# Three edits to a one-core layer kernel: per-tile score waits, expert groups in pairs on one ring of copy places, split products from chunk 6

## The chip, the cores and the metric

The kernel runs on one core of a Trainium2 chip. The core has five engines that run their own instruction queues in order: TensorE (PE), VectorE (DVE), ScalarE (ACT), GpSimd (POOL) and SyncE (SP), which here only issues transfers. The metric is the device time of one execution in microseconds (us).

## What is computed

A transformer layer for 4 batches of 128 tokens with 512 features: cross-attention to a context of 2048 rows of 384 features per batch, causal self-attention with 16 heads over low-rank projections, then a mixture of experts (4 shared blocks and 16 routed experts, 4 per token), each with a residual. Cut to what the change touches:

```python
query = einsum('bqi,ih->bqh', x, Wq) + bq
key   = einsum('bkt,th->bkh', ctx, Wk) + bk
value = einsum('bkt,th->bkh', ctx, Wv) + bv
weights = softmax(einsum('bqh,bkh->bqk', query, key) / sqrt(512))
x = x + einsum('bqk,bkh->bqh', weights, value)
# ... self-attention, then for each token its 4 experts e with weights c_e:
x = x + shared(x_norm) + sum(c_e * down_e(relu(up_e(x_norm)) ** 2))
```

The kernel folds Wk into the query and Wv behind the sum, so that scores are products with the context itself, and the second product is weights by context.

## The kernel before, in words

**Cross-attention.** The context comes in G = 16 chunks of 512 rows (4 per batch), each twice: transposed (`ring_T`, 4 places, three tiles t = 0, 1, 2 of 128 x 512) for the scores, and as it lies (`ring`, 3 places) for the product with the weights. One loop, written out alike on every engine, runs steps 1 to 20. In step s, chunk s is prepared, the scores of chunk s-1 are computed, and chunk s-5 (LAG = 5) goes through its second product. "Split" operands are a high part, rounded by a copy to the type float32r, and a low part, the rest; a split product is three matmuls (`split_mm`, L1580).

- ACT makes the high parts of a chunk (`chunk_hi`, L747) and DVE the low ones (`chunk_lo`, L1281); in steps 2 to 4 POOL makes the low part of tile 2 (L614). PE (`chunk_scores`, L1846) waits for all low parts of the chunk, then runs 9 matmuls. DVE moves the scores out (L1392), ACT takes the exponential (`chunk_weights`, L826).
- PE turns the weights (`chunk_T`, L1843) into bank B_W, ACT copies that to `wT` (L894, two places), and PE multiplies `wT` by `ring` in plain fp32 (L1898), four products per chunk.
- From step 8 on the same loop carries the work of finished batches: the normalised sums and their projection (`sums_hi`, `sums_lo`, `attended`), norms (`cross_added`, `normalise`, with a root on POOL, L598 and L620), `compress`, `keys_and_queries`, `values`. From step 13 (U_STEP) on it carries one self-attention unit per step: `pair_scores` (L1726, two units at a time), mask and maximum on DVE (`mask_and_max`, L1092 to L1100), `unit_exp` on ACT (L852), `unit_weights` on POOL (L627), `unit_T` on PE (L1748, into B_W too) and `unit_copy` on ACT (L841). In step 17, ACT and DVE also split the output weights W_O (L734, L1055).

The order of each engine's calls within a step is that of its loop: ACT at L880, DVE at L1352, PE at L1868, POOL at L642, the loads of SP at L507.

**Experts.** NG = 20 groups of 4 slots of 32 tokens. For each group PE turns the gathered tokens (`group_rows_T`, L2012), runs the up products (`group_up`, L2043), turns the hidden values (`group_hidden_T`, L2054) and runs the down products (`group_down`, L2075). Up and down products run as four column strips of 32, the transposes on the whole array. From group 4 (GS) on the experts are chosen at run time; the weights of slots 1 to 3 are first copied to fixed places, 4 for up and 4 for down (slots 1 and 2 by DVE, L1507 and L1514; slot 3 by ACT, L1016 and L1024). PE's loop (L2091) runs, per group, up(g), hidden_T(g-1), rows_T(g+2), down(g-2). At the end `last_shared` (L2086), 32 matmuls (L2113, L2114) and DVE's sums (L1559, L1563) close the output.

Of the kernel before, what the change touches and what calls it, by code (L numbers as in the profile page):

```python
# [36 lines left out]
def layer_program(nc, x, ctx_in, ctxT_in, wqT, wkT, wv, wd, wu, woT, experts, bq, bk, bv, gate, bias_e,  # L37
# [41 lines left out]
    with ExitStack() as es:  # L79
# [99 lines left out]
        ring_T = at("ring_T", [P, RING_T, TC, CHUNK], ring_at + RING * KT * TD * 4)  # L179
        sc = at("sc", [P, 2, NKEY], s_at)  # L180
# [69 lines left out]
        NC = 4  # L250
        up_copy = [at(f"up_copy{i}", [P, HALF], xT_at + i * HALF * 4) for i in range(NC)]
        down_copy = [at(f"down_copy{i}", [P, HALF], (ring_at, hw_at)[i // 2] + i % 2 * HALF * 4) for i in range(NC)]
# [106 lines left out]
        ulo_first, dlo_first = sem("ulo_first"), sem("dlo_first")  # L359
        u_lo_pool, d3_in = sem("u_lo_pool"), sem("d3_in")  # L360
# [51 lines left out]

        def pool_parts(g):
            return sum(q <= g for q in POOL_LO)
# [30 lines left out]
        def copy_no(g, q):  # L445

            return (NQ - 1) * (g - GS) + q - 1

        def place(g, q):
            return copy_no(g, q) % NC  # L450

        def last_user(g, q):

            n = copy_no(g, q) - NC
            return GS + n // (NQ - 1) if n >= 0 else None
# [5 lines left out]
        def _(sp):  # L461
# [19 lines left out]
            def load_chunk_T(g):  # L481
                if g >= RING_T:
                    sp.wait_ge(cTlo_ok, low_parts(g - RING_T))
                    if pool_parts(g - RING_T):
                        sp.wait_ge(cTlo_pool, pool_parts(g - RING_T))
                sp.dma_start(ring_T[:, g % RING_T], ctxT_in[g].rearrange("p (t n) -> p t n", t=TC)).then_inc(ctxT_at[g % RING_T], 16)
# [33 lines left out]
            load_expert(0)  # L520
            load_expert(1)
# [49 lines left out]
        def _(pool):  # L571
# [157 lines left out]
        def _(act_e):  # L729
# [17 lines left out]
            def chunk_hi(g, t):  # L747
                if t == 0:
                    act_e.wait_ge(ctxT_at[g % RING_T], 16 * (g // RING_T + 1))
                if g >= 2 and t == 0:  # L750
                    act_e.wait_ge(s_mm, g - 1)
                copy(cT[:, g % 2, 0, t, :], ring_T[:, g % RING_T, t, :]).then_inc(cThi_ok, 1)  # L752
# [75 lines left out]

            def attended_hi(b):
# [50 lines left out]
            for step in range(1, TAIL):  # L880
# [9 lines left out]
                if 0 <= g < G:  # L890
                    act_e.wait_ge(wT_mm, g + 1)
                    if g >= 2:
                        act_e.wait_ge(o_mm, g - 1)
                    copy(wT[:, g % 2, :], bank[B_W][:]).then_inc(wT_ok, 1)  # L894
# [113 lines left out]
            def copy_up(g, expert):  # L1008
                q = NQ - 1
                if g == GS:  # L1010
                    act_e.wait_ge(up_mm, IC * NSH)
                    for i in range(GS):
                        act_e.wait_ge(wx_in[i], 16 * NQ)
                if (v := last_user(g, q)) is not None:
                    act_e.wait_ge(hs_up, v + 1)
                copy(up_copy[place(g, q)][:], WX[:, bass.ds(expert * (2 * HALF), HALF)]).then_inc(up_third, 1)  # L1016

            def copy_down(g, expert):
                q = NQ - 1
                if g == GS:  # L1020
                    act_e.wait_ge(acc_mm, NSH - 1)
                if (v := last_user(g, q)) is not None:
                    act_e.wait_ge(ys_mm, v + 1)
# [1144 lines left out]
```

## Time and profile before

| | us |
|---|---|
| median of 3 runs (lowest, highest) | 355.23 (354.63, 355.56) |
| the profiled execution | 355.39 |
| its span, first to last instruction | 353.7 |
| PE busy in the span | 336.4 (95%) |
| DVE busy | 240.7 (68%) |
| ACT busy | 189.4 (54%) |
| POOL busy | 95.6 (27%) |

The mean granted TensorE clock is 0.99 of full speed. Busy PE time counts a matmul from its start to its modelled end, and ends overlap the next starts; what a matmul costs in a row of them is the distance between starts. The chunk loop's 20 steps lie between about 36 and 160 us, the groups of the experts between 248 and 340 us.

### The profile page before, as it was taken

Reading aid. Unit: us, or ns where it says so; the run is one execution under the profiler, and the core shown is the slowest. Engines: PE = TensorE matmul, PEld = TensorE weight load, DVE = VectorE, ACT = ScalarE, POOL = GpSimd, SP = SyncE. Lnnn points to the kernel's source line nnn. Section 1 sums busy time; section 2 is a strip of 40 time slices with the busy share of each in tenths; the row PEclk is TensorE's granted clock in tenths of the full one; section 3 lists DMA queues with packets and bytes.
Section 4 is the critical chain, followed back from the end, with each engine's and each line's share of the span. In section 5 each row is a group of like instructions: output and inputs, shape, how many; then the busy total and the mean of one; then the engine's idle time right before and its main releaser. Section 6 shows DMA issues by size and latency. Waiting matters only on the chain.

```text
span 353.7 us, 7041 instructions
## 1 busy us (share of the span) xinstructions
PE 336.4 (95%) x2554; PEld 235.2 (67%) x2554; DVE 240.7 (68%) x475; ACT 189.4 (54%) x428; POOL 95.6 (27%) x114
## 2 busy tenths in 40 slices
PE   6999889999999999999899899999999999999996
PEld 4998656677777766767789789787544444444344
DVE  2875869665489728748975469980547777778486
ACT  2356666533577476565777454402246777777520
POOL 3600310000001311226575140004457544432000
PEclk9899999999999999999899999999999999999999
DMA  6984398985333227118023470799835633321663
GB/s 232 400 336 165 139 396 356 418 290 216 120 126 111 92 90 259 69 39 348 0 89 124 149 267 16 294 380 391 341 110 184 196 120 120 121 92 61 238 268 119
DMA packets 17185, 69.70 MB, mean 197 GB/s; under 512 B 2816, under 2 KB 3328, under 8 KB 14592
## 3 DMA queue, kind: packets, MB, share of 16 engines
q1 hardware_dynamic: 12768, 56.93, 43.0%
q0 software_dynamic: 3520, 11.54, 9.4%
q10 hardware_dynamic: 864, 0.79, 0.7%
q8 instruction: 21, 0.34, 0.4%
q14 instruction: 12, 0.10, 0.1%
HBM read 61.91 MB, written 7.34 MB: 196 GB/s over the span
## 4 chain that ended last, share of the span: by engine, by line
PE 76%; DVE 12%; ACT 6%; issue 3%; DMA 2%; POOL 0%; ACTq 0%; DVEq 0%
PE bank L2075 10%; PE bank L2043 10%; PE bank L1582 8%; PE bank L1898 8%; PE bank L1584 8%; PE bank L1583 8%; PE bank L2012 3%; PE bank L1791 2%; PE bank L2054 2%; PE bank L2086 2%; DMA raw<-in_wkT 2%; DVE cT L1283 2%; PE bank L1748 2%; PE bank L1843 2%; PE bank L1589 1%
## 5 line engine op out<-in xcount | busy, mean ns | idle before, releaser
L1898 PE MATMUL bank<-ring,wT 128*128 128x384 f32 x128 | 44.0, 487 | 0.7 <-ACT wT L894 0.7
L2075 PE MATMUL bank<-WX,hsT 128*32 128x512 f32 (+1 forms) x128 | 38.2, 598 | 0.0
L2043 PE MATMUL bank<-WX,xsT 128*32 128x256 f32 (+1 forms) x256 | 37.9, 380 | 0.0
L1283 DVE TENSOR_TENSOR cT<-ring_T,cT 128x512 fp32r<-128x512 f32 x45 | 31.0, 732 | 6.7 <-ACT cT L752 6.7
L1898 PEld LDWEIGHTS bank<-ring,wT 128*128 128x128 f32 x128 | 23.6, 190 | 14.2 <-ACT wT L894 0.9
L2043 PEld LDWEIGHTS bank<-WX,xsT 128*32 128x32 f32 x256 | 17.9, 110 | 21.0 <-issue 10.7
L1514 DVE COPY down_copy<-WX 128x1024 f32 x32 | 21.0, 695 | 15.8 <-PE bank L2075 15.8
L2075 PE MATMUL bank<-down_copy,hsT 128*32 128x512 f32 x192 | 30.7, 598 | 0.0
L752 ACT CAST cT<-ring_T 128x512 fp32r<-128x512 f32 x48 | 27.0, 619 | 6.5 <-PE bank L1584 6.3
L2043 PE MATMUL bank<-up_copy,xsT 128*32 128x256 f32 x384 | 30.4, 379 | 0.0
L688 POOL DMA_INDIRECT xs<-x_rows,from_row x20 | 20.0, 1001 | 37.1 <-DVE to_row L1237 25.2
L598 POOL TENSOR_TENSOR rstd<-var,mhalf 128x1 f32<-128x1 f32 x12 | 7.5, 626 | 72.3 <-DVE var L1069 72.3
L695 POOL DMA_INDIRECT y_rows<-ys,to_row x16 | 17.1, 1068 | 33.7 <-ACT ys L1000 33.7
L1507 DVE COPY up_copy<-WX 128x1024 f32 x32 | 21.1, 696 | 7.4 <-PE bank L2043 3.5
L1024 ACT COPY down_copy<-WX 128x1024 f32 x16 | 16.8, 1049 | 17.1 <-PE bank L2075 17.1
L1492 DVE COPY xsT<-bank 128x512 f32<-128x512 f32 x20 | 13.7, 685 | 14.8 <-PE bank L2012 14.8
L1582 PE MATMUL bank<-cT,qk_h 128*128 128x512 f32 x48 | 20.2, 420 | 2.4 <-DVE cT L1283 1.7
L1016 ACT COPY up_copy<-WX 128x1024 f32 x16 | 16.8, 1048 | 4.7 <-PE bank L2043 3.4
L1584 PE MATMUL bank<-cT,qk_l 128*128 128x512 f32 x48 | 18.8, 392 | 0.0
L1583 PE MATMUL bank<-cT,qk_h 128*128 128x512 f32 x48 | 18.8, 392 | 0.0
L2075 PEld LDWEIGHTS bank<-WX,hsT 128*32 128x32 f32 x128 | 7.4, 109 | 16.5 <-issue 16.5
L1582 PE MATMUL bank<-xT_l,u_w 128*128 128x256 f32 (+2 forms) x56 | 17.9, 320 | 0.0
(296 smaller groups left out, 892.3 us busy)
## 6 DMA issues: line engine op xcount, KB each, us to landing
WX<-in_experts SPq DMA_DIRECT2D x16, 1024.0 KB, 7.0
ring_T<-in_ctxT SPq DMA_DIRECT2D x16, 768.0 KB, 6.8
ring<-in_ctx SPq DMA_DIRECT2D x16, 768.0 KB, 5.0
WX<-y_rows SPq DMA_DIRECT2D x4, 1024.0 KB, 9.4
raw<-in_experts SPq DMA_DIRECT2D x3, 1024.0 KB, 4.8
raw<-in_wqT SPq DMA_DIRECT2D x4, 256.0 KB, 5.6
res<-in_x SPq DMA_DIRECT2D x4, 256.0 KB, 7.8
raw<-in_woT SPq DMA_DIRECT2D x1, 1024.0 KB, 4.9
```

The costliest lines, as they stand in the source:

```text
L688: nc.gpsimd.indirect_dma_start(out=xs[:, s % NXS, :], out_offset=None, in_=x_rows, in_offset=bass.IndirectOffsetOnAxis(ap=from_row[:, s:s ...
L695: nc.gpsimd.indirect_dma_start(out=y_rows, out_offset=bass.IndirectOffsetOnAxis(ap=to_row[:, s:s + 1], axis=0), in_=ys[:, s % NYS, :], in_ ...
L752: copy(cT[:, g % 2, 0, t, :], ring_T[:, g % RING_T, t, :]).then_inc(cThi_ok, 1)
L1283: V_.tensor_tensor(cT[:, g % 2, 1, t, :], ring_T[:, g % RING_T, t, :], f32(cT[:, g % 2, 0, t, :]), ALU.subtract).then_inc(cTlo_ok, 1)
L1507: V_.tensor_copy(up_copy[place(g, q)][:], WX[:, bass.ds(expert * (2 * HALF), HALF)]).then_inc(up_copied, 1)
L1514: V_.tensor_copy(down_copy[place(g, q)][:], WX[:, bass.ds(expert * (2 * HALF) + HALF, HALF)]).then_inc(down_copied, 1)
L1582: mm(dst, a[0], b[1], start=start, stop=False)
L1583: mm(dst, a[0], b[0], start=False, stop=False)
L1584: return mm(dst, a[1], b[0], start=False, stop=stop)
L1898: last = mm(bank[B_O][:, 0:TD], wT[:, g % 2, k * P:(k + 1) * P], ring[:, g % RING, k, :], start=(c == 0 and k == 0), stop=(c == NCH - 1 an ...
L2043: last = mm(bank[B_H[g % 2]][q * SLOT:(q + 1) * SLOT, 0:IC * P], xsT[:, g % 2, c * P + q * SLOT:c * P + (q + 1) * SLOT], w, start=c == 0, ...
L2075: last = mm(bank[B_Y[g % 2]][q * SLOT:(q + 1) * SLOT, :], hsT[:, g % 2, m * P + q * SLOT:m * P + (q + 1) * SLOT], w, start=m == 0, stop=m ...
```

## The change

- **Scores.** PE waits before each of the three tiles for that tile's low part alone. In steps 2 to 4 POOL makes tile 0 in place of tile 2, as soon as its high part is there.
- **Second product.** From chunk 6 (SPLIT) on it runs on split operands: ACT makes the high part of the context chunk one step ahead (`context_hi`, two copies of 128 x 768), POOL the low part in place (`context_low`, two), ACT's copy of `wT` becomes the high part of the weights, and DVE makes their low part (`weights_lo`). `wT_r` has one place instead of two, and what writes B_W next waits for `weights_lo`. The high parts lie in the raw buffer and in the fourth place of `ring_T`, which has three places from chunk 8 on; SP loads expert 1 only after the product of chunk 14.
- **Experts.** PE runs up(g), up(g+1), rows_T(g+2), hidden_T(g), hidden_T(g+1), rows_T(g+3), down(g), down(g+1). The eight copy places form one ring in the order up pair, down pair; a place waits for the user eight copies earlier. ACT and DVE are reordered to match.

```diff
-                pool.wait_ge(cThi_ok, TC * (g + 1))
-                nc.gpsimd.tensor_tensor(cT[:, g % 2, 1, TC - 1, :], ring_T[:, g % RING_T, TC - 1, :], f32(cT[:, g % 2, 0, TC - 1, :]),
+                pool.wait_ge(cThi_ok, TC * g + 1)
+                nc.gpsimd.tensor_tensor(cT[:, g % 2, 1, 0, :], ring_T[:, slot_T(g), 0, :], f32(cT[:, g % 2, 0, 0, :]),
...
+            def context_low(g, h):
+                pool.wait_ge(ctxhi_ok, 2 * (g - SPLIT) + h + 1)
+                k = slice(h * HALF_KT, (h + 1) * HALF_KT)
+                nc.gpsimd.tensor_tensor(ring_lo[:, g % RING, k, :], ring[:, g % RING, k, :], f32(ctx_hi(g)[:, k, :]),
+                                        ALU.subtract).then_inc(ctxlo_ok, 1)
             for step in range(1, TAIL):
+                g = step - LAG + 1
+                if SPLIT <= g < G:
+                    context_low(g, 0)
                 if (b := batch_at(step, POST + 1)) is not None:
                     inverse_root(norm_no["middle", b])
...
                     unit_weights(u)
+                if SPLIT <= g < G:
+                    context_low(g, 1)
...
+            def context_hi(g):
+                act_e.wait_ge(ctx_at[g % RING], 16 * (g // RING + 1))
+                if g >= SPLIT + 2:
+                    act_e.wait_ge(o_mm, g - 1)
...
+                for h in range(2):
+                    k = slice(h * HALF_KT, (h + 1) * HALF_KT)
+                    copy(ctx_hi(g)[:, k, :], ring[:, g % RING, k, :]).then_inc(ctxhi_ok, 1)
...
+                    if g >= SPLIT:
+                        act_e.wait_ge(o_mm, g)
+                        copy(wT_r[:, 0, :], bank[B_W][:]).then_inc(wT_ok, 1)
...
+                if SPLIT <= g + 1 < G:
+                    context_hi(g + 1)
                 if (b := batch_at(step, POST)) is not None:
                     sums_hi(b)
...
+            def weights_lo(g):
+                dve.wait_ge(wT_ok, g + 1)
+                V_.tensor_tensor(wT_r[:, 1, :], bank[B_W][:], f32(wT_r[:, 0, :]), ALU.subtract).then_inc(wTlo_ok, 1)
...
                     chunk_lo(step, 1)
...
+                if SPLIT <= step - LAG < G:
+                    weights_lo(step - LAG)
                 if (b := batch_at(step, POST + 1)) is not None:
                     cross_added(b)
...
                     for t in range(TC):
+                        if g in POOL_LO and t == 0:
+                            pe.wait_ge(cTlo_pool, pool_parts(g))
+                        else:
+                            pe.wait_ge(cTlo_ok, low_parts(g) - TC + t + 1)
                         last = split_mm(bank[s_bank(g)][:], (qk_h[:, t, tok(b)], qk_l[:, t, tok(b)]),
...
+                        pe.wait_ge(ctxlo_ok, 2 * (g - SPLIT) + k // HALF_KT + 1)
+                        o = slice(k * P, (k + 1) * P)
+                        last = split_mm(bank[B_O][:, 0:TD], (wT_r[:, 0, o], wT_r[:, 1, o]),
+                                        (ctx_hi(g)[:, k, :], ring_lo[:, g % RING, k, :]), first, final)
...
+            for g in range(0, NG, PAIR):
+                if g >= GS:
+                    copy_up(g + 1)
+                if g > 0:
+                    group_results(g - 1)
+                group_hidden(g)
+                if g >= GS:
+                    copy_down(g)
+                group_hidden(g + 1)
+                group_hidden_T(g)
+                group_hidden_T(g + 1)
+                if g >= GS:
+                    copy_down(g + 1)
+                if GS <= g + 2 < NG:
+                    copy_up(g + 2)
+                group_results(g)
+            group_results(NG - 1)
...
+            for g in range(0, NG, PAIR):
+                group_up(g)
+                group_up(g + 1)
...
+                if g + 2 < NG:
+                    group_rows_T(g + 2)
+                else:
+                    last_shared(0)
+                group_hidden_T(g)
+                group_hidden_T(g + 1)
+                if g + 3 < NG:
+                    group_rows_T(g + 3)
+                else:
+                    last_shared(1)
+                group_down(g)
+                group_down(g + 1)
```

## Rows read from the trace of the kernel before

**Rows 1.** The page: the span.
```profile
span 353.7 us, 7041 instructions
```
**Rows 2.** Windows: stretch, length, then busy us (instructions) per engine, PEclk, DMA, GB/s.
```profile
97.00:160.00 63.00, 59.86 (x364) 44.05 (x363) 42.88 (x92) 39.32 (x122) 11.00 (x13) 1.00 0.33 114
```
**Rows 3.** The chain that ended last, in order of time: start, us, what.
```profile
132.06 1.81 ACT wo_w L734
```
**Rows 4.** Timeline, steps 2 to 5: start, us, engine, line, operation, count, [idle before].
```profile
37.10 1.04 ACT L734 CAST DW<-raw 128x1024 fp32r<-128x1024 f32 x1
...
38.78 1.66 ACT L752 CAST cT<-ring_T 128x512 fp32r<-128x512 f32 x3 [0.63 <-PE bank L1584]
...
40.31 2.38 DVE L1283 TENSOR_TENSOR cT<-ring_T,cT 128x512 fp32r<-128x512 f32 x2
...
40.52 1.63 POOL L616 TENSOR_TENSOR cT<-ring_T,cT 128x512 fp32r<-128x512 f32 x1 [1.95 <-ACT cT L752]
...
42.75 0.50 PE L1582 MATMUL bank<-cT,qk_h 128*128 128x512 f32 x1 [0.62 <-DVE cT L1283]
...
46.29 0.72 ACT L826 ACTIVATE sc<-sc,xnb 128x512 f32<-128x512 f32 x1 [0.50 <-DVE xnb L1397]
```
**Rows 5.** Timeline of PE: eight split matmuls in a row, and one plain second product.
```profile
14.99 0.34 PE L1612 MATMUL bank<-wk,UW 128*128 128x386 f32 x1
...
16.39 0.27 PE L1589 MATMUL bank<-ident,xn 128*128 128x128 f32 x1
...
124.22 2.75 PE L1898 MATMUL bank<-ring,wT 128*128 128x384 f32 x8
...
126.81 1.02 PE L1797 MATMUL bank<-wu_s,cf 128*128 128x512 f32 x2
```
**Rows 6.** Groups of POOL by shape: count, busy us, mean ns, idle before.
```profile
L639 POOL TENSOR_TENSOR u_w<-raw,u_w 128x512 fp32r<-128x512 f32 x4 | 5.1, 1276 | 0.0
...
L683 POOL TENSOR_TENSOR u_w<-raw,u_w 128x1024 fp32r<-128x1024 f32 x1 | 2.4, 2403 | 0.0
```
**Rows 7.** Timeline, steps 13 to 15.
```profile
97.90 1.29 DVE L1283 TENSOR_TENSOR cT<-ring_T,cT 128x512 fp32r<-128x512 f32 x2 [1.69 <-ACT cT L752]
...
98.77 0.49 ACT L835 CAST DW<-bank 128x384 fp32r<-128x384 f32 x1
...
105.60 0.59 ACT L894 COPY wT<-bank 128x512 f32<-128x512 f32 x1 [1.07 <-PE bank L1843]
...
110.93 1.16 PE L1738 MATMUL bank<-qk_s 32*128 32x128 f32 x16 [0.27 <-ACT hw L852]
```
**Rows 8.** Timeline, step 15.
```profile
118.44 0.73 DVE L1348 TENSOR_SCALAR cqn<-bank,mv,rstd 128x128 f32<-128x128 f32 x2 [0.81 <-POOL rstd L620]
...
119.23 0.44 PE L1779 MATMUL bank<-ident,cqn 128*128 128x128 f32 x2
```
**Rows 9.** Timeline, step 17, the output weights W_O.
```profile
131.94 1.92 ACT L734 CAST wo_w<-raw 128x2048 fp32r<-128x2048 f32 x1
...
133.89 2.29 DVE L1055 TENSOR_TENSOR wo_w<-raw,wo_w 128x2048 fp32r<-128x2048 f32 x1 [0.25 <-ACT wo_w L734]
```
**Rows 10.** Timeline of PE, one group of the experts.
```profile
263.78 0.38 PE L2043 MATMUL bank<-WX,xsT 128*32 x1
...
264.11 0.44 PE L2054 MATMUL bank<-ident,hs 128*128 128x128 f32 x2
264.38 0.60 PE L2012 MATMUL bank<-ident,xs 128*128 128x128 f32 x4
264.91 1.92 PE L2075 MATMUL bank<-WX,hsT 128*32 128x512 f32 x16
266.65 0.38 PE L2043 MATMUL bank<-WX,xsT 128*32 x1
```
**Rows 11.** Timeline of DVE, the end.
```profile
337.52 0.75 DVE L1535 SCALAR_TENSOR_TENSOR ys_l<-bank,s_cw,ys_h 128x512 fp32r<-128x512 f32 x1 [0.95 <-ACT ys_h L1000]
...
350.52 0.69 DVE L1563 TENSOR_TENSOR res<-res,bank 128x512 f32<-128x512 f32 x1 [0.22 <-PE bank L2114]
```

More of the change, by code:

```diff
@@ L482, in load_chunk_T @@
                 if g >= RING_T:
[L483 to L486, printed above, removed]
+                    v = max(q for q in range(g) if slot_T(q) == slot_T(g))
+                    sp.wait_ge(cTlo_ok, low_parts(v))
+                    if pool_parts(v):
+                        sp.wait_ge(cTlo_pool, pool_parts(v))
+                sp.dma_start(ring_T[:, slot_T(g)], ctxT_in[g].rearrange("p (t n) -> p t n", t=TC)).then_inc(ctxT_at[slot_T(g)], 16)
             def load_item(n, src, cols):
@@ L748, in chunk_hi @@
                 if t == 0:
-                    act_e.wait_ge(ctxT_at[g % RING_T], 16 * (g // RING_T + 1))
+                    act_e.wait_ge(ctxT_at[slot_T(g)], 16 * (1 + sum(slot_T(q) == slot_T(g) for q in range(g))))
                 if g >= 2 and t == 0:
                     act_e.wait_ge(s_mm, g - 1)
-                copy(cT[:, g % 2, 0, t, :], ring_T[:, g % RING_T, t, :]).then_inc(cThi_ok, 1)
+                copy(cT[:, g % 2, 0, t, :], ring_T[:, slot_T(g), t, :]).then_inc(cThi_ok, 1)
             def squares(e):
@@ L1006, in third_of, with place_free, copy_up @@
                 return nc.values_load(slot_expert[0:1, d:d + 1], engines=[mybir.EngineType.Activation], min_val=0, max_val=NE - 1)
-            def copy_up(g, expert):
-                q = NQ - 1
+            def place_free(n):
+                down, v = last_user(n)
+                if v is not None:
+                    act_e.wait_ge(ys_mm if down else hs_up, v + 1)
+            third = {}
+            def copy_up(g):
+                n = up_no(g, NQ - 1)
                 if g == GS:
                     act_e.wait_ge(up_mm, IC * NSH)
+                    act_e.wait_ge(acc_mm, NSH - 1)
@@ L1012, in copy_up @@
                     for i in range(GS):
                         act_e.wait_ge(wx_in[i], 16 * NQ)
[L1014 to L1023, printed above, removed]
-                copy(down_copy[place(g, q)][:], WX[:, bass.ds(expert * (2 * HALF) + HALF, HALF)]).then_inc(down_third, 1)
@@ L1355, in _ @@
                 if 1 < step < G:
-                    chunk_lo(step, 0)
+                    if step not in POOL_LO:
+                        chunk_lo(step, 0)
                     chunk_lo(step, 1)
-                    if step < U_STEP and step not in POOL_LO:
+                    if step < U_STEP:
                         chunk_lo(step, 2)
+                if SPLIT <= step - LAG < G:
+                    weights_lo(step - LAG)
                 if (b := batch_at(step, POST + 1)) is not None:
@@ L1498, in middle_of, with place_free, copies_up @@
                 return values
-            def copy_up(g, q, expert):
-                if g == GS and q == 1:
+            def place_free(n):
+                down, v = last_user(n)
+                if v is not None:
+                    dve.wait_ge(ys_mm if down else hs_up, v + 1)
+            middle = {}
+            def copies_up(g):
+                if g == GS:
                     dve.wait_ge(up_mm, IC * NSH)
@@ L2041, in group_up @@
                         else:
-                            w = up_copy[place(g, q)][:, o:o + IC * P]
+                            w = copies[up_no(g, q) % NC][:, o:o + IC * P]
                         last = mm(bank[B_H[g % 2]][q * SLOT:(q + 1) * SLOT, 0:IC * P],
```

153 lines of the change are left out of this document (84 added, 69 removed).

## The prediction

> **What bounds the kernel now.** I read the page first: the span is 353.7 us [rows 1], and the profiled execution took 355.39, so 1.7 lie around the span. My sum starts from 355.39; the median of the runs is 0.16 lower. Then I read busy time by stretch. In the chunk loop's second half, 97 to 160 us, PE is busy for 59.86 of 63.00 us [rows 2], so all its waits together are some 3 us. DVE at 42.88 and ACT at 39.32 look free, but a busy share doesn't tell that: both run long chains in which each waits for the other. The chain of waits tells it. Its rows leave PE in three places: in steps 2 to 5, in steps 13 to 15, and in step 17, where the longest is ACT's split of W_O [rows 3, 4, 7, 9]. Everywhere else PE is followed. Among the experts PE runs without a wait: up, hidden_T, rows_T, down and the next up follow each other directly, 4.4 us a group [rows 10].
>
> So three stages have to be costed: the start of the loop, where PE waits for low parts; its second half, where PE and the DVE-ACT loop are nearly tied; and the experts, where only PE counts.
>
> **Scores per tile, steps 2 to 5.** In step 3, ACT's casts run from 38.78 to 40.44, POOL's low part of tile 2 from 40.52 to 42.15, and the scores start at 42.75 after 0.62 of wait for DVE's low part [rows 4]. The two DVE subtractions beside POOL took 2.38 us, the same pair without POOL 1.29 [rows 4, 7]: 1.09 of hold. After the change POOL starts when the first cast is done, two casts (1.04 us) earlier. Followed through steps 2 to 4 with these durations, the scores of chunk 4 end about 2.5 us earlier. Then the exponential sets the end: it waits for DVE's maximum of the first batch and moves from 46.29 to some 45.6, and PE, which ran the scores after that, turns the weights directly behind it. PE enters the product of step 5 about 1.5 us earlier. From there to step 10 PE is the bound, so the gain stays. Bounds: 0 (POOL's tile is now the first that PE needs) and 2.5. I take **-1.5**.
>
> **The split product: PE.** A plain product takes 124.22 to 126.81, 2.59 us per chunk. Eight split matmuls of 386 columns start 14.99 to 16.39, 0.175 each; twelve are 2.10 [rows 5]. That is 0.49 saved per chunk, 4.9 on ten chunks if PE were the bound in all of them.
>
> By the Trainium skill (TensorE: Matmul & The Clock Gate, section "Back-to-back issue gap") a matmul of N columns takes N/2.4 + 2.5 ns when the clock is at its higher level, 162.5 ns here. The row is slower, 0.175. By the page a split product would be an estimated 1.95 us, and my sum, in which five steps keep the saving, would come out 0.7 us lower.
>
> **The split product: the other engines.** ACT gets two casts of 768 columns: one of 1024 is 1.04, three of 512 are 1.66 [rows 4], so each costs some 0.75, 1.5 per chunk. DVE gets one subtraction from the bank, 0.65 (half of the pair's 1.29). POOL gets two subtractions of 768: 1.28 for 512 and 2.40 for 1024 [rows 6] give 1.84, 3.7 per chunk on a step of some 7 us. What stands behind them decides:
> - Steps 10 and 11: POOL's root for a norm now stands behind a 1.84 us subtraction. In step 10 the product still covers it; in step 11 PE waits 0.3 more. The load of chunk 6 is also needed a step earlier and issued later (SP waits behind a `ring_T` load that has one place less); I add 0.3. **+0.6**.
> - Step 12: PE is the bound. **-0.45**.
> - Steps 13 and 14: ACT's `context_hi` stands ahead of `sums_hi` (98.77), DVE waits for that in `sums_lo`, and behind it are mask, `unit_exp`, the next casts and low parts. Then `weights_lo` stands ahead of `cross_added` on DVE, and waits for the copy that ends at 106.19. This loop ends in `pair_scores` at 110.93, for which PE waits for ACT already [rows 7]: nothing covers it. 1.45 + 0.65 = **+2.1**. The PE time saved on two products here is lost in that wait.
> - Step 15: `weights_lo` (0.65) stands ahead of the mask and `moments_2`, and POOL's second half holds one `chunk_lo` for some 0.25. cqn ends at 119.17 and PE uses it at 119.23 [rows 8]: no cover. **+0.9**.
> - Step 16: PE is the bound, -0.45; step 17: `unit_T` waits for `weights_lo`, +0.6, and the product gives 0.5 back. Together **-0.35**.
> - Steps 17 to 18: `context_hi` (1.5) stands ahead of W_O on ACT; DVE's low part of W_O (133.89, 2.29 long) waits for that [rows 9], POOL's second half holds it for 0.5 to 0.9, and then `weights_lo` of step 18 stands ahead of `cross_added`. 1.5 + 0.65 + 0.65 = **+2.8**.
> - Steps 19 and 20: no chunk preparation is left; of two savings about one reaches the end, as ACT's chain is as long. **-0.45**.
>
> The middle sums to +5.15. It can't be less than -4.9. The first loads of the ring have room: SP's wait for the product of chunk 14 ahead of expert 1 delays that load by some 18 us, but ACT needs it only at about 161 us, and behind it SP waits for the product of chunk 15 anyway.
>
> **Experts in pairs.** In one group, going from the last up wave to hidden_T costs 0.33 against 0.22 for a wave; the two hidden transposes take 0.27 against 2 x 0.11 (four take 0.60 with a last one of 0.27); four rows_T and the switch to down take 0.53 against 0.44; down takes 1.74 [rows 5, 10]. About 0.28 of the 4.39 is the price of changing between strips and the whole array and back. A pair pays it once: 10 x 0.28 = **-2.8** on PE. For the copies I laid a pair (8.5 us) out: the tightest are ACT's, which become free only when a down product ends and are needed 0.4 us after they end. So they don't stall PE. At the end, `last_shared(1)` (1.85) moves ahead of down(18). DVE's last chain starts behind down(18) at 337.52 and takes 13.7 us to the end of the row at 350.52, 351.21 [rows 11]. Now down(18) ends 2.8 - 1.85 = 0.95 earlier, and ACT has no copy (1.1) ahead of its result: the chain starts 2.1 earlier, and sets the end in PE's place. So **-2.1** of the 2.8 arrives.
>
> **Sum.** -1.5 + 5.15 - 2.1 = +1.55: 355.39 + 1.55 = 356.94 for the profiled execution, 356.8 against the median. I give **356.7**.
>
> **The rivals.**
> - *PE keeps the lead.* If the DVE-ACT loop of steps 13 to 15 has more room than its rows show, the +3.0 there falls away and two savings (1.0) stay: 356.7 - 4.0 = 352.7. For it: PE is 95% busy. Against it: PE's wait for ACT at 110.93. Chance 0.24. If W_O hides too, all ten savings stay: 355.4 - 1.5 - 4.9 - 2.1 = 346.9, chance 0.06.
> - *POOL holds DVE (slower).* Place: `chunk_lo` in steps 10 to 15. If POOL's subtraction is running when DVE starts one, DVE is held by up to 1.09 [rows 4, 7]. Six steps at 1.1, of which 0.9 is in the sum, give +5.6: 362.3. It decides from the point at which `context_low` of a step reaches the next step's `chunk_lo`. Against it: in most steps DVE has passed them by then. Chance 0.10.
>
> The Trainium skill (GPSIMD Engine Reference, section "1. Specifications") says that GpSimd shares its SBUF interfaces with VectorE and contends with instructions that have two SBUF inputs. The trace agrees: 2.38 against 1.29 us for the pair.
>
> - *Copies miss their place.* 0.4 us of room is small; 0.5 late in each of the eight pairs that copy is +4: 360.7. Chance 0.08.
> - *The scores don't start earlier*, as the first tile is now POOL's: 358.2. Chance 0.06.
>
> **How the numbers follow.** The forecast's chance is 0.46, with its own range 355.3 to 358.5. A measurement of this kernel can tell 0.3% (1.07 us) from no change, so the borders are 354.2 and 356.3. Faster: 0.22 + 0.06 = 0.28. Same: 0.16 of the forecast and 0.02 of the first rival, 0.18. Slower: 0.30 + 0.24 = 0.54. The range reaches from 352.0 to 360.8, and leaves out the full saving, the held DVE and little more.
>
> **What would show it.** Right: the first product starts near 47.7 and not 49.2; a pair of groups takes 8.5 us; `pair_scores` of step 15 follows `unit_exp` and comes late relative to step 12; DVE is idle ahead of `sums_lo` and `cross_added`; the step with W_O is the longest. Wrong: PE runs steps 13 to 18 without waits; DVE's subtractions of 512 columns take over 1 us on the mean; PE waits for a copy among the experts.

## The result, and the profile after

The changed kernel takes 362.35 us (median of 4 runs, 361.10 to 365.87) against 355.29 for the kernel before: a ratio of 1.022, 95% interval 1.0191 to 1.0248. The forecast was 356.7 with a range up to 360.8. The direction was right, the size was not: 7 us were lost, not 1.4. Where some runs of a kernel are over 1.5% slower than its fastest, medians and ratios go by the others; that holds for one kernel below, the one without ACT's casts (three of ten runs, its profiled execution among them).

The profiled execution took 362.23 us, 6.84 more than the one of before. Where they lie is read from the same event in both timelines: the first matmul of the weights-by-context product of each step, and the first up product of the experts. The view is PE's timeline (start, us, engine, line, operation, count, idle before). Five of the 17 starts, first of the kernel before:

```profile
49.23 2.85 PE L1898 MATMUL bank<-ring,wT 128*128 128x384 f32 x8 [0.68 <-ACT wT L894]
...
78.13 2.74 PE L1898 MATMUL bank<-ring,wT 128*128 128x384 f32 x8
...
116.44 2.75 PE L1898 MATMUL bank<-ring,wT 128*128 128x384 f32 x8
...
154.99 2.75 PE L1898 MATMUL bank<-ring,wT 128*128 128x384 f32 x8
...
248.35 1.93 PE L2043 MATMUL bank<-WX,xsT 128*32 128x256 f32 x32
```

and of the changed kernel:

```profile
47.19 2.85 PE L1983 MATMUL bank<-ring,wT 128*128 128x384 f32 x8 [0.67 <-ACT wT L942]
...
76.07 0.48 PE L1983 MATMUL bank<-ring,wT 128*128 128x384 f32 x1
...
121.37 0.34 PE L1658 MATMUL bank<-ring_lo,wT_r 128*128 128x384 f32 x1
...
162.24 0.42 PE L1658 MATMUL bank<-ring_lo,wT_r 128*128 128x384 f32 x1
...
255.48 0.85 PE L2133 MATMUL bank<-WX,xsT 128*32 128x256 f32 x12
```

These are the products of steps 5, 10, 15 and 20 and the first up product. In the table each term of the forecast stands in the stretch in which PE meets it: what a product saves, and the waits for `cqn` in steps 11 and 15, lie behind the start of that step's product, so that the forecast's steps and these stretches don't coincide.

| stretch | before, us | after, us | difference | forecast |
|---|---|---|---|---|
| to the product of step 5 | 49.23 | 47.19 | -2.04 | -1.5 |
| product of step 10 to that of 11 | 6.95 | 8.61 | +1.66 | +0.3 (the load) |
| 11 to 12 | 7.34 | 7.54 | +0.20 | +0.3 (the root of step 11) |
| 12 to 15 | 24.02 | 29.15 | +5.13 | +1.65 (-0.45, +2.1) |
| 15 to 17 | 14.66 | 15.17 | +0.51 | +1.05 (+0.9, -0.45, +0.6) |
| 17 to 20 | 23.89 | 25.70 | +1.81 | +1.85 (-0.5, +2.8, -0.45) |
| 20 to the first up product | 93.36 | 93.24 | -0.12 | 0 |
| first up product to the end | 105.30 | 105.01 | -0.29 | -2.1 |

Between the products of steps 5 and 10 both take 28.9 us. So the stretch from step 10 to the experts lost 9.19 where the sum had 5.15, and the experts gave 0.29 where it had 2.1. Two stretches hold the loop's miss: step 10 to 11 with 1.36 more than forecast, and 12 to 15 with 3.48 more; the others came out as forecast or shorter. The busy time by stretch tells a part of it (columns as in [rows 2], whose stretch is the first line here):

```profile
97.00:160.00 63.00, 54.27 (x346) 46.95 (x346) 44.74 (x90) 44.26 (x119) 34.21 (x25) 0.92 0.26 93
...
112.00:118.00 6.00, 5.74 (x29) 4.79 (x30) 4.29 (x10) 3.40 (x8) 0.14 (x1) 0.50 0.13 53
...
136.00:139.00 3.00, 3.00 (x12) 3.00 (x12) 2.10 (x5) 3.00 (x6) 3.00 (x3) 0.50 0.00 0
```

PE was busy for 59.86 of these 63 us and is now for 54.27; POOL went from 11.00 to 34.21. The granted clock was 1.00 in the whole stretch before; now it stands at 0.50, its lower level (1.2 GHz), from 112 to 118 and from 136 to 139. The two places where PE first waits show by what. The timeline of step 10, POOL, DVE and PE:

```profile
75.41 0.15 DVE L1128 TENSOR_SCALAR var<-mv 128x1 f32<-128x1 f32 x1
75.57 1.82 POOL L666 TENSOR_TENSOR ring_lo<-ring,ctx_hi_even 128x768 fp32r<-128x768 f32 x1 [32.82 <-ACT ctx_hi_even L871]
77.36 0.54 POOL L619 TENSOR_TENSOR rstd<-var,mhalf 128x1 f32<-128x1 f32 x1
77.88 1.80 POOL L666 TENSOR_TENSOR ring_lo<-ring,ctx_hi_even 128x768 fp32r<-128x768 f32 x1
78.01 1.95 DVE L1138 TENSOR_SCALAR xn<-res,mv,rstd 128x512 f32<-128x512 f32 x1 [2.44 <-POOL rstd L619]
...
80.02 0.33 PE L1665 MATMUL bank<-ident,xn 128*128 128x128 f32 x1 [1.21 <-DVE xn L1138]
```

The root waits for the first half of `context_low`, and the normalisation `xn` runs beside the second. Its median is 0.55 us; here it takes 1.95 and ends at 79.96, 0.28 after POOL's subtraction. In 0.55 us it would have ended at 78.56, before PE was ready at 78.81 (80.02 less the wait of 1.21): the product covers the root's delay, and it is the hold on `xn` that PE waits for. Step 14, the same engines:

```profile
106.69 1.84 POOL L666 TENSOR_TENSOR ring_lo<-ring,ctx_hi_even 128x768 fp32r<-128x768 f32 x1 [3.93 <-ACT ctx_hi_even L871]
107.44 0.70 DVE L1126 BATCH_NORM_STATS2 stats<-res 128x6 f32<-128x512 f32 x1
...
108.62 0.55 POOL L619 TENSOR_TENSOR rstd<-var,mhalf 128x1 f32<-128x1 f32 x1
109.13 1.04 POOL L648 TENSOR_TENSOR hw<-hw,hrd 128x512 f32<-128x512 f32 x1
...
110.13 1.80 POOL L666 TENSOR_TENSOR ring_lo<-ring,ctx_hi_even 128x768 fp32r<-128x768 f32 x1
110.63 1.58 DVE L1138 TENSOR_SCALAR xn<-res,mv,rstd 128x512 f32<-128x512 f32 x1
...
112.27 1.12 PE L1665 MATMUL bank<-ident,xn 128*128 128x128 f32 x4 [2.84 <-DVE xn L1138]
```

The statistics of the same rows, beside POOL's first half, take their usual 0.70. But again `xn` ends 0.28 us after POOL's subtraction (112.21 and 111.93). PE stands for 2.84 us, and when it goes on, its clock is at the lower level: four transposes take 1.12 us here, 0.66 at the higher one. In steps 17 and 18 PE waits for `weights_lo`:

```profile
135.83 0.43 PE L1826 MATMUL bank<-ident,hw 128*128 128x128 f32 x1 [1.17 <-DVE wT_r L1347]
...
144.15 0.63 PE L1826 MATMUL bank<-ident,hw 128*128 128x128 f32 x4 [1.49 <-DVE wT_r L1347]
```

The Trainium skill (SBUF — State Buffer, section "Who interferes with whom") says that a DVE `tensor_scalar` can enter a mode that takes the port pair shared with GpSimd, and that whichever of the two issued first then has it for its whole instruction while the other waits. The trace agrees here: POOL's subtraction started 0.13 and 0.50 us ahead, and `xn` took 1.95 and 1.58 us against 0.55. In the run with ACT's casts moved, below, `xn` starts first and is held as well, so that part on the order of issue isn't borne out there.

### The profile page after: what moved, and what is told of

Its sections match the earlier page's. It is cut to its first block, busy times and chain, and to the rows that moved or that the text cites. A ratio compares the mean times of both kernels' runs of the same rounds, so it can differ in the third digit from the quotient of the medians.

```text
span 360.5 us, 7190 instructions
## 1 busy us (share of the span) xinstructions
PE 333.3 (92%) x2594; PEld 245.0 (68%) x2594; DVE 248.5 (69%) x485; ACT 204.4 (57%) x448; POOL 135.4 (38%) x134
## 3 DMA queue, kind: packets, MB, share of 16 engines
HBM read 61.91 MB, written 7.34 MB: 192 GB/s over the span
## 4 chain that ended last, share of the span: by engine, by line
PE 62%; DVE 20%; ACT 7%; issue 4%; DMA 4%; POOL 1%; DVEq 0%; ACTq 0%; POOLq 0%
PE bank L2133 10%; PE bank L2165 9%; PE bank L1658 7%; PE bank L1660 7%; PE bank L1659 7%; PE bank L1983 4%; PE bank L2102 3%; DMA xs<-x_rows,from_row 2%; PE bank L1869 2%; DVE res L1635 2%; PE bank L1826 2%; PE bank L1923 2%; DVE cT L1342 2%; DMA raw<-in_wkT 2%; DVE xn L1138 2%
## 5 line engine op out<-in xcount | busy, mean ns | idle before, releaser
L720 POOL DMA_INDIRECT xs<-x_rows,from_row x20 | 22.7, 1134 | 49.1 <-DVE to_row L1296 25.2
L2165 PE MATMUL bank<-WX,hsT 128*32 128x512 f32 (+1 forms) x128 | 36.2, 595 | 0.0
L666 POOL TENSOR_TENSOR ring_lo<-ring,ctx_hi_even 128x768 fp32r<-128x768 f32 x10 | 18.2, 1828 | 44.2 <-ACT ctx_hi_even L871 44.2
L1582 DVE COPY copy<-WX 128x1024 f32 x32 | 20.8, 691 | 13.4 <-PE bank L2165 7.1
L2133 PE MATMUL bank<-copy,xsT 128*32 128x256 f32 x384 | 29.3, 381 | 0.0
L2165 PE MATMUL bank<-copy,hsT 128*32 128x512 f32 x192 | 29.1, 595 | 0.0
L666 POOL TENSOR_TENSOR ring_lo<-ring,ctx_hi_odd 128x768 fp32r<-128x768 f32 x10 | 18.3, 1839 | 20.5 <-ACT ctx_hi_odd L871 20.5
L1589 DVE COPY copy<-WX 128x1024 f32 x32 | 21.6, 715 | 5.9 <-PE bank L2133 3.8
L727 POOL DMA_INDIRECT y_rows<-ys,to_row x16 | 18.7, 1171 | 12.2 <-ACT ys L1050 9.4
L1074 ACT COPY copy<-WX 128x1024 f32 x16 | 16.8, 1048 | 8.4 <-PE bank L2165 7.2
L1659 PE MATMUL bank<-xT_h,u_w 128*128 128x256 f32 (+2 forms) x56 | 17.5, 312 | 0.0
L1660 PE MATMUL bank<-xT_h,u_w 128*128 128x256 f32 (+2 forms) x56 | 17.5, 312 | 0.0
```

The source lines that it names most:

```text
L666: nc.gpsimd.tensor_tensor(ring_lo[:, g % RING, k, :], ring[:, g % RING, k, :], f32(ctx_hi(g)[:, k, :]), ALU.subtract).then_inc(ctxlo_ok, 1)
L720: nc.gpsimd.indirect_dma_start(out=xs[:, s % NXS, :], out_offset=None, in_=x_rows, in_offset=bass.IndirectOffsetOnAxis(ap=from_row[:, s:s ...
L727: nc.gpsimd.indirect_dma_start(out=y_rows, out_offset=bass.IndirectOffsetOnAxis(ap=to_row[:, s:s + 1], axis=0), in_=ys[:, s % NYS, :], in_ ...
L1582: V_.tensor_copy(copies[n % NC][:], WX[:, bass.ds(middle[g][q - 1] * (2 * HALF), HALF)]).then_inc(up_copied, 1)
L1589: V_.tensor_copy(copies[n % NC][:], WX[:, bass.ds(values[q - 1] * (2 * HALF) + HALF, HALF)]).then_inc(down_copied, 1)
L1659: mm(dst, a[0], b[0], start=False, stop=False)
```

## The experiments

### The three parts, each alone on the kernel before

The change was taken apart into its three parts, each with its own names and lines as the diff has them.

**The split product alone.**

> Only the second part: the weights-by-context product on split operands from chunk 6. By the product starts of the changed kernel it costs 9.2 us between steps 10 and 20, and this adds to the time before: 364.5, with a granted clock of 0.5 behind PE's longest waits, in steps 14 to 15 and step 16. Rival, the sum on record: +5.15, so 360.4, the rest being an effect of the three parts together.

Measured: 364.19 us, ratio 1.0257 (1.0209 to 1.0305). The products from step 10 to the experts take 179.5 us, as in the changed kernel (179.4; 170.2 before), and the clock falls in the same places. The loss belongs to this part and needs neither of the others; the expected 364.5 came, the rival's 360.4 did not.

**The scores alone.**

> Only the first part of the change, on the kernel before: PE waits per context tile and POOL makes the low part of tile 0 in steps 2 to 4. If that part is what moved the first product of the loop from 49.23 to 47.19 us in the changed kernel, it does so here too, nothing later gives it back, and the time is 355.3 - 2.0 = 353.3. Rival, the size on record in the prediction: 1.5, so 353.8. Second rival: PE's lead runs into a transfer or into the DVE-ACT loop of steps 13 to 18 and the gain is lost there, 355.0 or more.

Measured: 354.63 us, ratio 0.9983 (0.9960 to 1.0005): no difference that can be measured. The time lies nearest to the second rival's, but the gain is lost in a place that it did not name. The first product starts at 47.03, and the product of step 20 is still 2.2 us early (152.81 against 154.99). But the experts begin only 0.7 early. The busy time by stretch of this kernel:

```profile
165.00:168.00 3.00, 3.00 (x37) 2.19 (x37) 2.61 (x5) 1.91 (x10) 1.56 (x2) 0.50 0.03 11
180.00:185.00 5.00, 5.00 (x54) 4.81 (x52) 4.61 (x9) 3.08 (x12) 4.96 (x5) 1.00 0.74 257
186.00:188.00 2.00, 2.00 (x34) 1.54 (x27) 1.54 (x5) 0.78 (x5) 1.04 (x1) 0.50 0.67 240
```

The clock is at the lower level twice between the loop and the experts; the kernel before has one such stretch there (0.50 from 167 to 169) and 1.00 from 185 to 188. The runs say the same: the one with a mean clock of 1.0 took 352.50, one with 0.995 took 352.98, those with 0.985 took 354.6 to 355.2. The kernel before took 353.88 to 354.21 in its runs with 0.999 to 1.0. At the same clock the part is worth 1.4 to 1.7, by that one run. That the clock takes the gain back is read from these rows and runs; no run holds the clock there to show it.

**The pairs alone.**

> Only the third part: expert groups in pairs with the ring of eight copy places. In the changed kernel a pair takes 8.51 us once and 8.56 to 8.90 afterwards, against 2 x 4.386 = 8.77 before, because 0.43 to 0.66 us pass between the last up product of a pair and the transposes of the rows behind it (0.31 in the first pair). If the same holds here, the gain is small: 0.3 to 0.8, so 354.5 to 355.0. Rival: those gaps come from what the second part left behind (a later start, other transfers); then a pair takes 8.51 here and the time is about 353.

Measured: 353.83 us, ratio 0.9960 (0.9943 to 0.9978), between the expected 354.5 and the rival's 353. From the first up product to the end 104.94 us pass (105.30 before), and nine pairs take 8.72 on the mean. A part of the better time lies ahead of the experts: the profile has no fall of the clock at 165. At a mean clock of 0.999 to 1.0 the runs took 353.46 to 353.81, some 0.4 less than the kernel before at that clock. The gaps are the same as in the changed kernel, so they are of the pairs' own making.

**The pairs with the register loads apart.**

```diff
                 group_up(g)
+                if GS <= g + 2 < NG:
+                    first_of(g + 2)
                 group_up(g + 1)
-                for n in (g + 2, g + 3):
-                    if GS <= n < NG:
-                        first_of(n)
+                if GS <= g + 3 < NG:
+                    first_of(g + 3)
```

> The third part with one edit: PE's two loads of an expert's number into a register stand one behind each up product instead of both behind the second one. Theory: two such loads in a row are what takes 0.12 to 0.35 us more than the 0.31 of the first pair, which has none; apart, each hides as one did in the kernel before, a pair takes 8.51 and the time falls by 8 x 0.25 = 2.0 against the pairs alone. Rival: the transposes wait for gathered rows or for a copied bank; then the gaps stay and the time is that of the pairs alone.

Measured: 352.54 us, ratio 0.9924 (0.9896 to 0.9953). PE's timeline around the last up product of the ninth pair, first with both loads behind it (the pairs alone):

```profile
320.03 0.38 PE L2130 MATMUL bank<-WX,xsT 128*32 x1
320.04 0.39 PE L2130 MATMUL bank<-copy,xsT 128*32 128x256 f32 x3
320.79 0.63 PE L2099 MATMUL bank<-ident,xs 128*128 128x128 f32 x4 [0.35 <-issue]
```

and with one behind each:

```profile
318.74 0.38 PE L2130 MATMUL bank<-WX,xsT 128*32 x1
318.75 0.39 PE L2130 MATMUL bank<-copy,xsT 128*32 128x256 f32 x3
319.07 0.66 PE L2099 MATMUL bank<-ident,xs 128*128 128x128 f32 x4
```

From the last product of the four strips to the transposes pass 0.73 us in the first and 0.31 in the second, and it is 0.31 in all nine pairs that have rows behind them; nine pairs take 8.54 on the mean. The theory held, with 1.3 us by the medians of the 2.0 that it expected; gathered rows and copies were never late.

### What makes the split product dear

**PE kept busy in the wait of step 14.**

```diff
                 if (b := batch_at(step, POST + 1)) is not None:
+                    if b == 1:
+                        pe.wait_ge(var_ok, norm_no["middle", b] + 1)
+                        for _ in range(24):
+                            nc.tensor.transpose(bank[B_POST][:, 0:P], ident[:], ident[:])
                     rows_T(norm_no["middle", b], bank[B_POST])
```

> The changed kernel with 24 added transposes of the identity on PE, in step 14 alone, between the end of the product (109.4 us) and the transposes of the rows (112.27), where PE waits 2.84 us and behind which the granted clock is 0.5 until 118.5. They write a bank that the row transposes overwrite. Nothing is made earlier by them. Theory: the wait costs a second time through the clock, so with PE busy in it the clock stays at 1.0, the product of step 15 starts some 2.7 us earlier (118.7 and not 121.4) and the time falls from 362.3 to 359.6. Rival: the late step 15 is the chain of DVE and ACT alone; then 362.3 or more.

Measured: 361.90 us, ratio 1.018 (1.0140 to 1.0220). In the profile the place does what the theory says:

```profile
112.00:118.00 6.00, 5.76 (x51) 5.01 (x50) 5.87 (x10) 4.23 (x13) 2.19 (x2) 1.00 0.35 131
...
114.53 0.66 PE L1665 MATMUL bank<-ident,xn 128*128 128x128 f32 x4 [0.24 <-DVE xn L1138]
...
124.27 0.44 PE L1857 MATMUL bank<-ident,cqn 128*128 128x128 f32 x2 [1.34 <-DVE cqn L1411]
```

The clock stays at its higher level (2.4 GHz), and from the product of step 14 to that of step 15 pass 11.34 us in place of 14.31: 2.97 less, with nothing made earlier on any other engine by the edit itself. Of this, 0.84 goes again in step 15, where PE now waits 1.34 us for `cqn`; in the changed kernel it is 0.50:

```profile
124.15 0.44 PE L1857 MATMUL bank<-ident,cqn 128*128 128x128 f32 x2 [0.50 <-DVE cqn L1411]
```

From the product of step 14 to that of step 20, 2.14 are left (53.04 against 55.18). The median moved by only 0.45. The profiled execution, 362.82 us, lost the gain in another place, step 10:

```profile
75.70 1.57 ACT L871 CAST ctx_hi_even<-ring 128x768 fp32r<-128x768 f32 x2 [1.11 <-DMA ring<-in_ctx]
...
81.04 0.66 PE L1665 MATMUL bank<-ident,xn 128*128 128x128 f32 x4 [2.40 <-DVE xn L1138]
```

ACT waited for the load of chunk 6, PE then for `xn`, and the clock fell there (step 10 to 11: 11.18 us, against 8.61). The edit stands in step 14 alone, so this is not its doing: in four of the ten profiled executions with a split product ACT waited for this load, 0.48 to 1.77 us, and in three of them step 10 to 11 took 11.2 us. Two other runs of this kernel, with a mean clock of 0.990 and 0.995, took 360.98 and 360.14. The price of the clock in step 14 is shown; a gain of the whole kernel is not.

**POOL's low parts behind the normalised rows.**

```diff
-                if SPLIT <= g < G:
+                rows = batch_at(step, POST + 1)
+                if SPLIT <= g < G and rows is None:
                     context_low(g, 0)
...
                 if SPLIT <= g < G:
+                    if rows is not None:
+                        pool.wait_ge(xn_ok, norm_no["middle", rows] + 1)
+                        context_low(g, 0)
                     context_low(g, 1)
```

> The changed kernel with one edit on POOL: in steps 10, 14 and 18 both halves of the low part of the context stand behind the normalised rows and not ahead of the root and beside them. Theory: POOL's second half holds DVE's normalisation (1.95 and 1.58 us in steps 10 and 14, against 0.55 without) and its first half delays the root. Then those rows take 0.55 us, PE's wait of 1.21 us in step 10 goes, that of step 14 falls from 2.84 to some 1.8, and the time falls by 1.4 + 1.0 = 2.4 to 359.9; if the clock then stays up in step 14, by 2.7 more, 357.2. Rival: the hold is covered by other late work and the time stays at 362.

Measured: 360.34 us, ratio 1.0164 (1.0128 to 1.0201). Step 10 to 11 takes 7.18 us (8.61), 14 to 15 takes 12.45 (14.31), `xn` takes 0.54, and PE waits 1.80 for it. The time is between the expected 359.9 and the rival's 362, nearer the first; its interval and that of the changed kernel just overlap. DVE's timeline shows where the rest went:

```profile
109.50 0.54 DVE L1142 TENSOR_SCALAR xn<-res,mv,rstd 128x512 f32<-128x512 f32 x1
...
110.62 1.86 DVE L1346 TENSOR_TENSOR cT<-ring_T,cT 128x512 fp32r<-128x512 f32 x1
...
113.00 2.30 DVE L1346 TENSOR_TENSOR cT<-ring_T,cT 128x512 fp32r<-128x512 f32 x2
...
110.11 4.04 POOL L666 TENSOR_TENSOR ring_lo<-ring,ctx_hi_even 128x768 fp32r<-128x768 f32 x2 [1.08 <-DVE xn L1142]
```

The moved subtractions now run beside `chunk_lo`, of which one takes 0.69 and two 1.28 in the changed kernel: 2.2 us of hold in place of 1.0.

**Both of them.** The edit above, and 14 added transposes in the wait of step 14.

> The changed kernel with POOL's low parts behind the normalised rows in steps 10, 14 and 18 (as in low_later) and 14 added transposes of the identity on PE in the wait of step 14, which was 1.80 us long in low_later. If the two causes add, from the product of step 14 to that of step 15 pass 12.45 - 1.6 = 10.8 us at a granted clock of 1.0 (8.95 in the kernel before, 14.31 in the changed one), the products of steps 15 to 20 keep that, and the time is 358.5 or less, against 360.3 for low_later. Rival: with the hold gone, the fall of the clock in step 14 is covered by DVE's and ACT's chain; then 12.4 and 360.3.

Measured: 360.91 us, ratio 1.0167 (1.0123 to 1.0210): the time of the rival, by a mechanism that it did not name. The clock is 1.00 from 97 to 136, and yet from product 14 to 15 pass 13.67 us:

```profile
113.07 3.96 DVE L1346 TENSOR_TENSOR cT<-ring_T,cT 128x512 fp32r<-128x512 f32 x2
116.95 0.68 DVE L1351 TENSOR_TENSOR wT_r<-bank,wT_r 128x512 fp32r<-128x512 f32 x1
...
117.77 0.63 PE L1830 MATMUL bank<-ident,hw 128*128 128x128 f32 x4 [2.60 <-DVE wT_r L1351]
```

PE is now early, ACT casts the next context early, POOL's next subtraction starts at 114.52 between two `chunk_lo`, and the pair takes 3.96 us instead of 1.28. `weights_lo` stands behind them, and PE waits 2.60 for it. So the two causes don't add: `low_later` and this kernel each put POOL's 1.8 us beside other instructions of DVE. And with no fall of the clock in the loop at all, the ten steps from 10 to 20 still take 84.87 us here, against 86.17 in the changed kernel and 76.86 before: most of the loss can stand without the clock.

**ACT's casts behind the exponentials, alone and with the edit on POOL.** `context_hi(g + 1)` moves from ahead of `sums_hi` to behind `chunk_weights`.

> The changed kernel with one edit on ACT: the casts of the context stand behind the exponentials of the chunk weights and not ahead of the casts of the sums, the third tile and those exponentials. Theory: these 1.57 us per step are what makes the chain of DVE and ACT in steps 13 to 14 and 17 late; behind the exponentials ACT waits 1.5 us and more for DVE anyway. Then PE's wait in step 14 falls by 1.5 and the time by 1.5 to 360.8, and by up to 2.7 more if the clock stays up. Rival: the chain is made late by the subtraction of the weights on DVE and by POOL; then the time stays, or rises because POOL's low parts come later and PE waits for them.

> The changed kernel with both edits: POOL's low parts behind the normalised rows in steps 10, 14 and 18, and ACT's casts of the context behind the exponentials of the chunk weights. act_later alone lost 2.3 us: the casts no longer stood in the chain, but POOL's subtractions then ran beside two low parts of tiles in step 14 (2.09 us for the pair against 1.29) and ahead of the root. Theory: the hold on DVE, not the order on ACT, decides; with the root freed, step 14 loses its 3.46 us of wait, but the pair of low parts stays held by 0.8. Then 360.3 - 1.5 + 0.8 = 359.6, about the time of low_later. Rival: the order on ACT is worth its 1.5 us in steps 13 to 14 and again in step 17 once the root is free; then 357.5.

Measured: 364.70 us, ratio 1.0245 (1.0195 to 1.0296), and with the edit on POOL 361.67, ratio 1.0173 (1.0139 to 1.0208). Alone it got slower, as its rival allows, but PE did not wait for POOL's low parts: POOL's subtractions start later and stand ahead of the root and beside `xn` and two `chunk_lo`. (Its profiled execution is the slowest of the four, 366.93 us; the load of chunk 6 was late in it, and step 10 to 11 took 11.22.)

```profile
106.99 2.09 DVE L1342 TENSOR_TENSOR cT<-ring_T,cT 128x512 fp32r<-128x512 f32 x2 [0.77 <-ACT cT L784]
...
113.51 2.19 DVE L1138 TENSOR_SCALAR xn<-res,mv,rstd 128x512 f32<-128x512 f32 x1
...
115.75 0.48 PE L1665 MATMUL bank<-ident,xn 128*128 128x128 f32 x2 [3.46 <-DVE xn L1138]
```

Here `xn` starts 0.10 us ahead of POOL's subtraction (113.61 to 115.42) and is held all the same, again to 0.28 us behind its end: which of the two started first doesn't decide which one waits. With both edits the time is above both numbers on record and within the noise of `low_later`: no worth of the order on ACT can be seen.

**Each engine's added work taken away.** POOL's, ACT's and DVE's part of the split are cut to one column, with their order, their waits and the count of PE's matmuls kept; each of these kernels leaves that part out of its products. For POOL:

```diff
-                nc.gpsimd.tensor_tensor(ring_lo[:, g % RING, k, :], ring[:, g % RING, k, :], f32(ctx_hi(g)[:, k, :]),
+                nc.gpsimd.tensor_tensor(ring_lo[:, g % RING, k, 0:1], ring[:, g % RING, k, 0:1], f32(ctx_hi(g)[:, k, 0:1]),
```

> The changed kernel with POOL's low part of the context cut to one column of each 384; PE reads the high part in its place, so the low part of the context is left out of the product, and every other instruction stands where it did. Takes away 3.7 us of POOL per step with what it holds. By the sum on record POOL's part is 0.6 + 0.25 + 0.65 = 1.5: 360.8. By the trace of the changed kernel it is 1.4 in steps 10 to 11, 1.0 in step 14 and 0.4 in step 17, and the fall of the clock behind the wait of step 14 (2.7): 356.8, with no wait in step 10 and 1.8 us in step 14.

> The changed kernel with ACT's casts of the context cut to one column of each 384; POOL subtracts the context from itself in the same length and PE reads that in place of the high part, so the context is left out of the products from chunk 6. By the sum on record ACT's part is 1.45 in steps 13 to 14 and 1.5 in step 17: 359.4; with a wait in step 14 too short for the clock to fall, 2.7 less, 356.7. Rival: POOL's subtraction then starts earlier or beside other instructions of DVE and holds those, as in act_later; then 362.

> The changed kernel with DVE's low part of the weights cut to one column; PE reads the high part in its place, so the low part of the weights is left out of the products from chunk 6. By the sum on record DVE's part is 0.65 in steps 13 to 14, 0.65 in step 15, 0.6 in step 17 and 0.65 in step 18: 2.55, 359.8; with the clock held in step 14 some 357. Rival: these 0.65 us lie in time that DVE waits for POOL or ACT anyway: 362.

| taken away | time, us | ratio to the kernel before | product of step 10 to that of 20, us |
|---|---|---|---|
| nothing (the changed kernel) | 362.35 | 1.0220 (1.0191 to 1.0248) | 86.17 |
| POOL's subtractions | 357.82 | 1.0104 (1.0047 to 1.0161) | 80.75 |
| ACT's casts | 357.75 | 1.0092 (1.0060 to 1.0123) | not comparable |
| DVE's subtraction | 362.13 | 1.0192 (1.0124 to 1.0259) | 85.60 |

POOL's part is 4.5 us of time by the medians, 4.1 by the ratios, which leave some 2 us of room, and 5.42 us of these ten steps in the two traces, the fall of the clock included. The expectation put it at 1.5 by the sum and at 5.5 by the trace of the changed kernel; strictly the sum had 1.2, since half of the 0.6 for steps 10 and 11 was the load of chunk 6. Without POOL's part PE has no wait for `xn` in step 10, and the clock is 1.00 throughout the loop, though PE still waits 1.80 us for `xn` in step 14:

```profile
112.00:118.00 6.00, 6.00 (x40) 5.58 (x39) 5.71 (x15) 5.21 (x16) 0.20 (x1) 1.00 0.01 3
...
109.50 0.66 PE L1665 MATMUL bank<-ident,xn 128*128 128x128 f32 x4 [1.80 <-DVE xn L1138]
```

What is left of the ten steps, 80.75 against 76.86 before, is +3.89; the sum without POOL's terms was 5.15 - 1.2 = 3.95. ACT's part is 4.6 us by the medians, as much as POOL's and between the 3.0 and 5.7 on record, but not ACT's alone: POOL's subtraction reads one tile there and takes 1.47 us in place of 1.84, and starts earlier. The profiled execution of this kernel took 361.74 us, so its steps don't show what its median is made of; how much of the 4.6 is ACT's stays open. DVE's is not settled. The time did not move, but in that execution ACT waited 1.14 us for the load of chunk 6, the clock fell in step 10, and step 10 to 11 took 11.18 us; from step 11 to 20 pass 74.42 against 77.56.

### The two other parts together

Scores and pairs, the register loads apart, without the split product.

> The first and the third part together, with the two register loads apart, and without the split product: what is left if the second part is the cause of the loss. The pairs with loads apart gave 352.5. If the gain of the scores is eaten by the granted clock as in the kernel with the scores alone (a clock of 0.985 in most runs, and 352.5 in the run with 1.0 against 354.6), the time is 352; if not, 352.5 - 2.0 = 350.5.

Measured: 352.21 us, ratio 0.9913 (0.9884 to 0.9943): 3 us faster than the kernel before and 10 faster than the changed one. Against the pairs with loads apart the scores add 0.3, not 2.0, which is the first number on record (352): the first product starts at 46.98, and the clock is at 0.50 from 165 to 168 and from 186 to 188, as in the kernel with the scores alone.

## Why the prediction was wrong

**The bound.** That the second half of the loop has some 3 us of slack and no more was right [rows 2]: the work that was put on ACT, DVE and POOL there made the loop longer.

**Scores: right.** From the first scores to the first product pass 14.27 us in place of 15.99: -1.72 against -1.5; 0.32 more was there before the scores begin. That this would reach the end was taken for granted ("PE is the bound, so the gain stays"). It holds as far as step 20; behind it, in the kernel with the scores alone, most of the gain goes where the clock falls once more than before.

**The product on PE: right.** Twelve split matmuls start 99.72 to 101.66 and the next operation at 101.83: 2.11 us, forecast 2.10.

**POOL: the term that was mis-sized, 1.2 for 5.4.** The 5.4 holds the clock's fall in step 14, the next point. The step that failed is the place of the hold: it was looked for at `chunk_lo` alone. No term of the sum is for the normalisation `xn`, so it stands there at its 0.55 us. But the second half of `context_low` stands behind the same root in POOL's queue, so the two run side by side in steps 10 and 14. That cost PE the 1.21 us of step 10 and 1.03 of the 2.84 in step 14. "In step 10 the product still covers it" was right for the root, which came 1.8 us late, with 0.25 to spare, and left out `xn`. W_O's low part was held too, 2.73 us against 2.29 [rows 9]: 0.44 where 0.5 to 0.9 stood.

**The clock: not in the sum at all.** The stretch had 1.00 throughout [rows 2], and every duration came from rows at that level. The wait in step 14 was in the sum, as 2.1 us for the chain of ACT and DVE; the time behind it, 2.97 us to the next product and 2.14 by step 20, which the added transposes give back, was not. In the kernel with both edits, where DVE's chain is held elsewhere, filling the wait gave nothing back.

**ACT and DVE: right.** In the kernel without POOL's part the ten steps are longer by 3.89 us, against 3.95 in the sum. By stretches it is +0.41 where 0.3 stood in steps 10 to 12, +1.68 for 1.65 in 12 to 15, +0.95 for 0.8 in 15 to 17, and +0.85 for 1.2 in 17 to 20. That the sums agree to 0.06 is luck, as differences of up to 0.35 cancel; the places are right too, but for two: in steps 10 to 12 the 0.3 stood for the load, which was not late in that execution, and in steps 13 and 14 PE meets the late chain at `xn`, not at `pair_scores`. How this part divides between ACT and DVE isn't shown.

**The load of chunk 6: right in the execution compared, not in others.** The sum gave it 0.3. In the changed kernel's profile ACT does not wait for it; in three others it does, and step 10 to 11 takes 2.6 us more, the clock's fall included.

**The pairs: the mechanism right, one instruction forgotten.** A pair without register loads takes 8.51 us, as forecast, and with the loads apart 1.99 us arrive at the end, against 2.1; DVE's chain ends last there, as forecast. But the edit also put two loads of a register in a row, 0.06 to 0.35 us a pair in the changed kernel, which no row of the trace shows as an instruction. Moving a step moves all that it issues.

**The rivals.** "POOL holds DVE" had the engine and nearly the time (362.3), but not the place: in the changed kernel `chunk_lo` has a median of 0.69 us and is not held in the loop's second half. What it describes is seen only in kernels in which the order on POOL or ACT was changed. "PE keeps the lead" fell: PE waits 1.21, 2.84, 1.17 and 1.49 us for DVE in steps 10, 14, 17 and 18. No copy among the experts was missed, and the scores did start earlier: those two fell too.

## What to carry to other kernels

Where a new instruction on POOL is released by the same event as one on DVE, look at what DVE runs beside it, and price the pair as one after the other, not only for the instructions that were seen held. In a stretch whose clock is at the higher level, a new wait of PE may cost twice: the wait itself, and the work behind it at the lower level. Not every such wait did here, so give the second price a chance and not a certainty. And in a reordered loop count the instructions that leave no row, register loads among them.

## What the hardware showed that was not expected

- DVE's `tensor_scalar` from SBUF to SBUF is held by a POOL subtraction to 0.28 us beyond its end (1.95, 1.58 and 2.19 us for 0.55, the last although it started 0.10 us ahead of POOL), while `bn_stats` of the same rows beside POOL's first half took its usual 0.70.
- One register load of PE between two products hides within 0.31 us; two in a row show as 0.35 to 0.73 from the last product to the next transposes.
- The clock fell behind a wait of PE of 2.84 us, but also at 185 us of the kernel with the scores alone, with PE busy in all of the 5 us before; and behind one of 1.80 it fell in one kernel (`low_later`, 0.68 from 110 to 115) and stayed in another (without POOL's part). Why was not found. The ten runs of the kernel with the scores alone go with it, from 352.50 us at a mean clock of 1.0 to 355.19 at 0.985.
